# The inverse transform of a spectral layer's columns, with the operands of the matrix multiply exchanged

## The reference

```python
x = coords @ fc0_w + fc0_b                          # (32, 64, 64, 3) -> 32 channels
x = jnp.transpose(x, (0, 3, 1, 2))
for sw, cw, cb in layers:                           # 4 layers
    x_ft = jnp.fft.rfft2(x, norm='ortho')
    out = jnp.einsum('bixy,ioxy->boxy', x_ft[:, :, :20, :20], sw)
    out_ft = zeros; out_ft[:, :, :20, :20] = out
    x1 = jnp.fft.irfft2(out_ft, s=(64, 64), norm='ortho')
    x2 = jnp.einsum('bchw,oc->bohw', x, cw) + cb
    x = gelu(x1 + x2)                               # exact gelu
x = gelu(transpose(x) @ fc1_w + fc1_b) @ fc2_w + fc2_b
# then: class token, layer norm, banded attention with 8 heads, top-6 of 64 experts, layer norm
```

## Time and profile before

| | us |
|---|---|
| median of 3 runs (lowest, highest) | 1164.38 (1162.56, 1165.36) |
| the profiled execution, own time | 1165.57 |
| its span in the profile | 1163.8 |
| TensorE busy (share of the span) | 1067.9 (92%) |
| TensorE weight loads busy | 710.2 (61%) |
| VectorE busy | 623.3 (54%) |
| ScalarE busy | 409.6 (35%) |
| GpSimd busy | 124.5 (11%) |

### The profile page before, as it was taken

The page is one execution under the profiler, slowest core; times in us unless marked ns, Lnnn a source line. Parts: engine busy times, 40 slices in busy tenths (PEclk is TensorE's granted clock), DMA queues, the critical chain, the costliest instruction groups (busy, mean ns, idle before and its releaser), DMA issues.

```text
span 1163.8 us, 34246 instructions
## 1 busy us (share of the span) xinstructions
PE 1067.9 (92%) x15860; PEld 710.2 (61%) x15860; DVE 623.3 (54%) x782; ACT 409.6 (35%) x554; POOL 124.5 (11%) x112
## 2 busy tenths in 40 slices
PE   5899999999999999999899999999999899678896
PEld 4577767767776633677677767767325788522221
DVE  2248445823844322458338545833144577789787
ACT  2332233133223386231232223123586777321100
POOL 6000000000000000000000000020000755211511
PEclk9999999999999999999999999999899999789999
DMA  5220130022012400310220031020011000000000
GB/s 182 87 73 3 36 110 17 2 87 73 3 39 64 131 6 24 111 30 3 87 73 2 13 119 31 3 87 16 2 24 41 2 2 1 1 1 1 5 5 10
DMA packets 25652, 46.62 MB, mean 40 GB/s; under 512 B 9437, under 2 KB 10488, under 8 KB 24869
## 3 DMA queue, kind: packets, MB, share of 16 engines
q1 hardware_dynamic: 24694, 43.49, 12.4%
q10 hardware_dynamic: 384, 0.66, 0.2%
q0 software_dynamic: 432, 0.29, 0.1%
HBM read 30.25 MB, written 10.89 MB: 35 GB/s over the span
## 4 chain that ended last, share of the span: by engine, by line
PE 74%; DVE 13%; ACT 3%; issue 3%; DMA 3%; POOL 2%; SPq 1%; ACTq 0%; POOLq 0%; DVEq 0%
PE PSALL L1221 22%; PE PSALL L1080 9%; PE PSALL L1189 7%; PE PSALL L1097 7%; DVE WORK L1413 5%; PE PSALL L1299 4%; PE PSALL L1212 4%; PE PSALL L1165 4%; PE PSALL L1309 3%; PE PSALL L494 2%; PE PSALL L397 2%; DVE WORK L949 2%; DMA WORK<-MIXED 2%; DVE WORK L1432 2%; PE PSALL L482 2%
## 5 line engine op out<-in xcount | busy, mean ns | idle before, releaser
L1432 DVE STREAM_TRANSPOSE WORK<-PSALL 128x1024 f32<-128x1024 f32 x128 | 152.4, 1229 | 319.6 <-PE PSALL L1189 319.6
L1221 PEld LDWEIGHTS PSALL<-EW,WORK 64*128 64x128 f32 x4096 | 250.5, 193 | 65.5 <-issue 48.4
L1221 PE MATMUL PSALL<-EW,WORK 64*128 64x128 f32 x4096 | 266.7, 283 | 12.8 <-DVE WORK L1432 12.8
L1349 ACT ACTIVATE X<-PSALL,TABLES 128x1024 f32<-128x1024 f32 x128 | 141.7, 1114 | 333.6 <-PE PSALL L1221 333.6
L1413 DVE STREAM_TRANSPOSE WORK<-PSALL 128x1024 f32<-128x1024 f32 x100 | 119.1, 1230 | 58.4 <-PE PSALL L1080 54.6
L1097 PE MATMUL PSALL<-TABLES,WORK 128*128 128x128 f32 x1000 | 138.4, 287 | 4.9 <-DVE WORK L1413 0.5
L1097 PEld LDWEIGHTS PSALL<-TABLES,WORK 128*128 128x128 f32 x1000 | 120.7, 194 | 32.1 <-issue 18.4
L1330 ACT COPY SPEC<-PSALL 128x400 f32<-128x400 f32 x64 | 53.5, 846 | 175.5 <-PE PSALL L1097 172.3
L1080 PE MATMUL PSALL<-WORK,DW 32*64 32x256 f32 x3200 | 103.3, 389 | 12.6 <-DMA B<-in_fc_b 12.6
L1409 DVE STREAM_TRANSPOSE WORK<-X 128x1024 f32<-128x1024 f32 x96 | 111.4, 1204 | 0.0
L949 DVE TENSOR_TENSOR WORK<-PSALL,X 128x832 f32<-128x832 f32 x80 | 80.4, 1019 | 16.6 <-PE PSALL L482 15.7
(11 more groups left out here) (146 smaller groups left out, 962.1 us busy)
## 6 DMA issues: line engine op xcount, KB each, us to landing
SW<-in_spec_w SPq DMA_DIRECT2D x160, 80.0 KB, 2.8
spec_scr<-MIXED SPq DMA_DIRECT2D x24, 400.0 KB, 3.3
SPEC<-spec_scr SPq DMA_DIRECT2D x32, 200.0 KB
WORK<-spec_scr SPq DMA_DIRECT2D x16, 200.0 KB
WORK<-MIXED SPq DMA_DIRECT2D x64, 40.0 KB
WORK<-in_coords_w SPq DMA_DIRECT2D x2, 1024.0 KB, 4.9
XC<-in_coords_c SPq DMA_DIRECT2D x2, 1024.0 KB, 7.2
hid_scr<-WORK SPq DMA_DIRECT2D x64, 8.0 KB
```

The costliest lines, as they stand in the source:

```text
L1221: m = pe.matmul(PS[2 * p + z][:, 2 * b * GRID:(2 * b + 2) * GRID], G[64 * z:64 * z + 64, n % 2, b, h:h + 4, :, c].rearrange("p q o -> p (q ...
L1349: nc.scalar.activation(X[:, n].rearrange("p b (z d) c w -> p d z b (c w)", z=2)[:, p, :, :, 2 * t * GRID:2 * (t + 1) * GRID], PSALL[:, 2 * ...
L1432: nc.vector.transpose(G[:, n % 2, 2 * x + y].rearrange("p h o v -> p o h v"), PSALL[:, 4 + 2 * x:6 + 2 * x, :].rearrange("p k (h o v) -> p ...
```

## The change

The inverse columns exchange their operands: the table EW is the weight (64 x 32), and the data G are streamed. TensorE takes the images one by one. The result comes out with its axes in blocks the wrong way round, so it goes to banks PS[6:8], and VectorE writes it by one block transpose, PSUM to PSUM, into the pair of banks that the image has in PS[0:4]. The pointwise multiply then adds to it, where before it came first; it takes 64 rows of the array instead of 32, with weights of which every other 32 rows are zero (`ODD`, and in layer 0 two masked copies of W0). Four multiplies with the identity (`arm`) replace `keep_busy`, so that later multiplies add to what VectorE wrote. `inverse_rows` does one image per call, two tiles of 64 x 64 side by side, into PS[4:6]. `columns(0)` stands behind the last pointwise, and two of the four `pixels_onto_partitions` that open a forward stage stand among the last images' transposes. `smx`, `emx` and `rden` of the tail move into E0's memory, and `TABLES` and `W0` grow.

```diff
-            def inverse_rows(l, n, y):
...
+            def arm():
+                for bank in range(4):
+                    pe.matmul(PS[bank], ident[:], work[:, 0:BANK], start=True, stop=True)
+
+            def inverse_rows(l, i):
+                n, y, x, b = place(i)
...
+                if i:
+                    turn.wait(g_ready, i)
+                for a, b, bank, at in ((0, 8, 4, 0), (8, MODES // 2, 5, 0)):
                     for z in range(2):
...
+                        m = pe.matmul(PSALL[64 * z:64 * z + 64, bank, at:at + (b - a) * 2 * CH],
+                                      TABLES[64 * x:64 * x + 64, l, EH0 + 64 * z:EH0 + 64 * z + 64],
+                                      MODE[n % 2][64 * x:64 * x + 64, y, a:b, :],
+                                      start=True, stop=True, tile_position=(64 * x, 64 * z))
...
+            def image_columns(i, z):
+                n, y, x, b = place(i)
+                for w in range(2):
+                    for q in range(4):
+                        m = pe.matmul(PS[6 + z][Q * q:Q * q + Q, :].rearrange("p (m h o) -> p m h o", h=2, o=CH)[:, :, w],
+                                      EW[64 * z:64 * z + 64, GRID + Q * w:GRID + Q * w + Q],
+                                      G[64 * z:64 * z + 64, n % 2, b].rearrange("p (m q) o v -> p q m v o", q=4)[:, q],
+                                      start=True, stop=True, skip_group_check=True, tile_position=(64 * z, Q * q))
...
+            def image_pointwise(l, i, z):
...
                 for p in range(2):
+                    for q in range(4):
+                        m = pe.matmul(PS[2 * (i % 2) + z][Q * q:Q * q + Q, 256 * p:256 * p + 256],
+                                      TABLES[row, l, ODD if p else 0:(ODD if p else 0) + CH] if l else W0[row, p, 4 * (image // OCT) + q, :],
+                                      X[row, n, b, q].rearrange("p c w -> p (c w)") if l else
+                                      XC[row, image % OCT].rearrange("p c w -> p (c w)"),
+                                      start=False, stop=True, skip_group_check=True, tile_position=(64 * z, Q * q))
...
                 mix()
-                pointwise(l, 0, 0)
-                keep_busy(3)
-                inverse_rows(l, 0, 0)
...
+                arm()
+                inverse_rows(l, 0)
+                inverse_rows(l, 1)
+                issue(image_columns(0, 0), image_columns(0, 1))
...
+                for i in range(GIMG):
+                    if i + 2 < GIMG:
+                        inverse_rows(l, i + 2)
+                    elif i + 1 < GIMG:
+                        turn.wait(g_ready, GIMG)
+                    turn.wait(t_ready, i + 1)
+                    if i + 1 < GIMG:
+                        issue(image_columns(i + 1, 0), image_columns(i + 1, 1))
+                    issue(image_pointwise(l, i, 0), image_pointwise(l, i, 1))
+                if l < LAYERS - 1:
+                    columns(0)
+                elif p + 1 < PASSES:
+                    first_columns_dft()
...
+            def inverse_columns_out(i):
+                turn.wait(ic_full, i + 1)
+                if i >= 2:
+                    turn.wait(x_ready, i - 1)
+                t = 2 * (i % 2)
+                nc.vector.transpose(PSALL[:, t:t + 2, :].rearrange("p z (m h w) -> p h (z m) w", h=2, w=Q),
+                                    PSALL[:, 6:8, :].rearrange("p z (m h o) -> p h (z m) o", h=2, o=CH)
+                                    ).then_inc(t_ready.sem, 1)
...
-                    for k in range(4):
+                    for k in range(2, 4):
                         pixels_onto_partitions(k)
...
+                inverse_rows_out(0)
+                for i in range(GIMG):
+                    if i + 1 < GIMG:
+                        inverse_rows_out(i + 1)
+                    inverse_columns_out(i)
+                    if l + 1 < LAYERS and i in (13, 14):
+                        pixels_onto_partitions(i - 13)
```

More of the change, by code:

```diff
@@ L1026, in layer @@
                     if n >= 2:
-                        turn.wait(ih_full, 2 * (n - 1))
+                        turn.wait(ih_full, 4 * (n - 1))
                     load_modes(n, loaded[n])
@@ L1038, in _ @@
                     if l == LAYERS - 1 and p + 1 < PASSES:
-                        turn.wait(ih_full, 6)
+                        turn.wait(ih_full, 12)
                         load_coords(p + 1)
@@ L1180, in inverse_rows @@
                     turn.wait(mix_ready, N_MIX)
                     turn.wait(straight_in, 1)
-                elif y == 0:
+                elif i % B4 == 0:
                     turn.wait(loaded[n], 1)
-                if n or y:
-                    turn.wait(g_ready, 4 * n + 2 * y)
-                for a, b in ((0, 8), (8, MODES // 2)):
+                if i:
+                    turn.wait(g_ready, i)
+                for a, b, bank, at in ((0, 8, 4, 0), (8, MODES // 2, 5, 0)):
                     for z in range(2):
[L1188 to L1192, removed]
@@ L1193, in inverse_rows @@
-                m.then_inc(ih_full.sem, 1)
[L1195 to L1238, removed]
-                for p in range(2):
[L1240 to L1245, removed]
@@ L1252, in layer, with issue @@
+            def issue(*parts):
+                for _ in itertools.zip_longest(*parts):
+                    pass
             def layer(p, l):
@@ L1256, in layer @@
                 mix()
-                pointwise(l, 0, 0)
-                keep_busy(3)
-                inverse_rows(l, 0, 0)
[L1260 to L1273, removed]
+                arm()
+                inverse_rows(l, 0)
+                inverse_rows(l, 1)
+                issue(image_columns(0, 0), image_columns(0, 1))
+                if l == 0:
+                    passes.wait(xc_in, 1)
+                for i in range(GIMG):
[11 more added lines that the diff above has]
+                    first_columns_dft()
             first_columns_dft()
@@ L1289, in _ @@
                 turn.wait(g_ready, 0)
+                turn.wait(t_ready, 0)
                 for m0 in range(GIMG + 1):
@@ L1569, in layout @@
     for l in range(LAYERS):
[L1570 to L1571 removed]
+        for odd, at in enumerate((0, ODD)):
+            table[:, l, at:at + CH].reshape(2, 2, CH, CH)[:, odd] = tok[f"cw{l}"].T
+            table[:, l, MARK + odd].reshape(2, 2, CH)[:, odd] = 1
+        table[:, l, BIAS] = np.tile(tok[f"cb{l}"], 4)
+        table[:, l, DH0:ODD] = rows[l]
     d["tables"] = table
```

84 lines of the change are left out of this document (42 added, 42 removed).

## The result

The changed kernel takes 1236.63 us (median of 4, 1232.71 to 1239.44) against 1164.87: slower by 6.1%, ratio 1.0612, 95% interval 1.0571 to 1.0653. The forecast was 1204, with 1186 to 1222 as its range. The direction was right and the size was half of the true one: 39 us against 72.

A forecast was written before the change was run, and what follows sets the result against it. The prediction took TensorE as the inverse stage's bound, with waits at its two ends. It summed 1165.57 + 30 + 3.5 + 1.0 + 0.3 + 5 = 1205.4, or 1204 us on the median's scale; range 1186 to 1222.

The forecast's parts named there:

- TensorE's time for an image: Steady inverse stage: columns, pointwise and one-image inverse rows sum to 3.20 us an image against 3.17, so no gain.
- d of a change of tiles: Cost on TensorE of changing the tiles, 0.22 us, or 0.15 at the inverse rows; assumed also between 64 x 64 and 64 x 32.
- the first rival: Changing between 64 x 64 and 64 x 32 tiles costs nothing: period 2.83 us, total 1165 or just under 1160; 8%.
- The gain of the columns: Inverse columns take 0.87 us an image instead of 2.02, a gain of 1.1 us, spent on pointwise and inverse rows.
- VectorE hidden: Steady part: VectorE's second transpose takes 1.23 us, its cycle 2.6 us, hidden under TensorE's 3.20.
- The second rival: The PSUM to PSUM transpose is slow: at twice 1.23 us the period is 3.82, total about 1290; 6%.
- the third: Inverse columns writing PSUM with gaps run at half rate, 0.87 us more an image, total about 1315; 5%.
- The ends: Stage ends: TensorE waits 0.9, 0.6 and 2.65 us; layers 0 to 2 5.0 us slower, layer 3 3.5 and 1.0.
- the structure: The change's cost outside the clock: 30 us for six layers, 3.5 and 1.0 for layer 3, 0.3 for tables.
- The clock: The new 2.65 us wait at seven places may halve TensorE's clock, 1.66 us a fall, 0 to 11.6; three falls, 5 us.
- the sign: Direction of the whole kernel's change: slower 93%, no change 3%, faster 4%.
- the start stays: Start of the inverse stage: the modes' DMA hides `arm`, 3.7 us, so the inverse rows begin no later.

The follow-up runs named there:

- the end fills: Changed kernel plus useless whole-array multiplies (512, 512, 256 columns) in the new 2.55 us wait between first columns and first rows, six places: 1207.3 us, 1.0353.
- the half fill: Changed kernel plus useless multiplies in the waits at the inverse stages' starts, on two 64 x 64 tiles in the array's upper half: 1215.49 us, 1.0397.

## Why the prediction was wrong, step by step

- **TensorE's time for an image**: right. 3.20 forecast, 3.15 measured; d of a change of tiles is paid between 64 x 64 and 64 x 32, so the first rival is out. The gain of the columns went where I said, into the inverse rows (1.22 us for one image instead of two) and the wider pointwise. Splitting the modes gave 0.52 us an image back.
- **VectorE hidden**: right, with the transpose at 1.232 and no wait in the steady part. The second rival (slow PSUM to PSUM) and the third (the columns' output with gaps) are out: the columns take 0.93 us. By the Trainium skill (SBUF — State Buffer, Door 1) an output with gaps should have slowed them significantly; with pieces of 32 values the trace shows no such thing.
- **The ends**: right, 58.8 us with a whole clock against 59.3 forecast, and 31 us for the structure against 34.8.
- **The clock**: the step that failed. "I take three falls, 5 us" should have been 14 falls and some 39 us: six starts of 4.3 and two of 2.5 make 31, and six ends of 1.4 make 8 (from `rows` to the next layer's first inverse rows it is 48.9 us, against 47.5 before). The two falls in the last layer of the first pass add 3 to 5 us more, the gap of 1.25 among them. Three things were wrong in it. I put the danger at the new wait at the end alone and took the starts over from before, where one in eight fell; with waits of the same length all eight did. I took the price of a fall from one row, 1.66 us, while here it lasts up to three times as long. And I took busy as busy: waits that mostly left the clock alone beside work on the whole array brought it down beside work on half of it, and it stayed down through work without a gap.

Outside the clock the mechanism stands, and so does the sign; the term of the clock was mis-sized by 34 us at these 14 places, with most of the cause at a place that I had ruled out ("the start stays"). The forecast missed by 33 and not by more because the structure, forecast 4 us too long, hid about as much as the two further falls added; that was luck.

What the traces show of the cause, by starts that fell: the waits beside inverse rows on the whole array, 1 of 8 (the kernel before); the same waits beside half of it, 8 of 8, for 6.8 or 10.2 us (the change); half of it with the waits for VectorE filled, 0 of 8 (with the ends filled too 1 of 8, for 13.7 us); the waits kept and the array filled for the first two images, 5 of 8, four of them for 3.4 us; the waits kept and the modes split, so rows on the whole array for 0.70 instead of 1.22 us, 7 of 8, all for 3.4 us. So filling the waits spares all the starts or all but one, the whole array alone does not, and falls of 10.2 us or more at a start stand only in kernels with half empty inverse rows.

What stays open: how the waits and the half empty array share the first fall, why the end fills spared four starts, and how far the moment of a start decides; the times of the half fill suggest that the falls also differ between executions of one kernel. The share of the half empty array at a start, with nothing else changed, was tested only through the first two images, since no bank is free for the others.

## What to carry to other kernels

A step that left half of TensorE's array empty cost twice here: once in columns, and again in the clock, because waits stood beside it. Before a stage is cut into smaller pieces, list each wait that TensorE has beside them, the old ones as well as the new, and price a fall of the clock for each; the shortest fall in the trace of before is not the upper bound (3.4 us there, up to 10.2 here and 13.7 in one run). And where an operand has a free axis, split that axis over the array's halves instead of giving each half another item: here this took the kernel from 6.1% over the kernel before to 1.2% under it.

## What the runs showed of the hardware

- The granted clock fell right behind 2.92 us of which TensorE was busy for 2.86, on half of the array, with a wait of 1.79 us ahead of them; with the whole array in the fill and the same wait it stayed. It stayed at 0.50 through 10.2 us of unbroken work.
- Useless multiplies on the whole array, 34 us in all by their busy time (4.3 a layer), made the kernel 39 us faster.
- A 128x1024 block transpose from PSUM to PSUM takes 1.232 us on VectorE, as from PSUM to SBUF (1.229).
- Tiles of the array's other half start beside earlier ones although they are issued behind them: 16 instructions took 1.24 us in one order and 1.25 in the other.
